# One-hots marked in batches of 16 and 20 groups of columns, and tables stored with one run per partition, in a graph network on one Trainium2 core

## The chip, the core and the metric

The kernel runs on one core of one Trainium2 chip. The core has five engines with a queue each: TensorE (PE, matmuls, with its weight loads listed as PEld), VectorE (DVE), ScalarE (ACT), GpSimd (POOL) and SyncE (SP), which here only issues DMAs. SBUF has 128 partitions. The metric is the device time of one execution in microseconds (us); the time before is a median of 3 runs.

## The reference

A graph of N = 6250 nodes with 128 values each has E = 206,250 directed edges (100,000 in both directions, and one from each node to itself). Two networks run one behind the other:

```
# first network, 2 layers (l = 0, 1); row, col = the edge's two ends
m   = relu(concat(h[row], h[col]) @ msg_W1[l].T + msg_b1[l]) @ msg_W2[l].T + msg_b2[l]
agg = segment_sum(m, col, num_segments=N)
h   = layer_norm(h + concat(h, agg) @ upd_W[l].T + upd_b[l])
# second network, 3 layers; src, dst = the edge's ends
agg = segment_sum(h[src], dst, num_segments=N) / max(deg, 1)
h   = agg @ Wl[i].T + bl[i] + h @ Wr[i].T          # relu between layers
```

Around each stand a layer norm of the input, a relu and a residual sum.

## The kernel before

The nodes lie in SBUF as 50 tiles of P = 125 rows: node t*125 + p is in partition p, tile t. First the edges are **sorted** (0 to 590 us) into slots: for a target tile, up to 32 x 13 slots in each of four row groups hold the edges whose target is there. Then come five edge stages, with short dense stages between them that make the next tables. `Fori` is a hardware loop; a semaphore makes an engine wait until a count is reached.

**Edge stages of the first network** (functions `cells_*`, lines L1190 to L1423; l = 0 from about 635 us, l = 1 from about 1411 us). Their source tables `TABH` lie in SBUF in float16. Each of the 50 target tiles is visited twice in a layer (h = 0 with 6 positions of slots, h = 1 with 7), 200 visits in all. For a visit SyncE loads the tile's lists of slots (`lists`, L1202) and the target rows of that tile (`stack`, L1208). VectorE compares lists with row numbers (`by_node`: L1395 for the 125 source rows into `toN`, L1396 for 64 rows that stand for target rows into `toB`) and slots with columns (`by_slot`, L1404). ScalarE copies the target rows into `cur` (`own_rows`, L1363). TensorE gathers (L1326 from `TABH`, L1330 from `cur`), ScalarE applies the relu (L1377), TensorE scatters (L1344) and VectorE adds the sums (L1412; `sums(0, ...)` for the first half of a visit's positions, `sums(1, ...)` for the second). `toB` and `cur` have 96 rows, of which 64 are used; GpSimd clears the other 32 at the start of each layer (L1276), and TensorE waits for that by `f_one`.

The target rows go through DRAM. While the last tables are made, in five blocks c of 10 tiles, SyncE stores for each block the target rows (L1220, to `rows_stacked`) and the source rows (L1222, to `table_a`, from which GpSimd later gathers the rare edges that found no slot). In block 2 it also loads the target rows of the first two tiles. Its queue is in order, so the lists of the third tile (L1202) are asked for after the stores of block 4.

**The first edge stage of the second network** (functions `linear_*` and `counts_dve` with l = 0, lines L1440 to L1656, 2214 to 2730 us). One iteration takes two target tiles, 100 cells of 125 x 125 (a cell: how many edges go from one source tile to the target tile). The 100 cells are 25 groups of 4 (`GROUP`, positions 0 to 24; tile u = 1 starts at position 12). For each group VectorE makes two one-hots of 4 x 126 columns (`onehots`, L1590, from `curS2` and the constants `col1` and `colg`), TensorE multiplies them to counts (`count`, L1518), ScalarE copies these to float16 (L1580), TensorE multiplies them with the table (`total`, L1538), and SyncE stores them for the two later layers (L1443). The one-hots have RING = 5 buffers of one group. After the last group of a tile VectorE takes the sums (`sums`, L1610, L1613, L1603): those of tile u = 1 at position 4 of the next iteration, those of u = 0 at position 17. GpSimd copies the slots of the next tile to `curS2` (`own_slots`, L1479 and L1481), gathers the rows of rare edges (`far_rows`, L1487 and L1489) that TensorE adds at positions 12 and 24 (`far_total`, L1526), and after its loop adds a bias to all of X for a later stage (L2133, five instructions). 

**The two later layers** (2772 to 3075 and 3108 to 3430 us) load the stored cells again; TensorE multiplies them with the table (L1551).

The functions that the change touches:

## Time and profile before

| what | value |
|---|---|
| median of the 3 runs (3422.79 to 3432.80) | 3429.53 us |
| profiled execution | 3434.72 us, of which the span of its instructions 3433.0 us |
| mean granted TensorE clock | 0.93 |
| PE / DVE / ACT / POOL busy | 86% / 75% / 60% / 18% of the span |
| first network, l = 0 and l = 1 | about 635 to 1320 us and 1411 to 2070 us |
| second network, l = 0, 1, 2 | 2214 to 2730, 2762 to 3076, 3107 to 3430 us |

Busy time is a union of instructions, and TensorE's matmuls overlap each other by most of their length; how fast an engine goes is read from the distance of starts. A releaser behind "<-" is what ended an engine's idle time; "issue" is idle time in which the profile shows nothing waited for.

### The profile page before, as it was taken

What the parts mean: (1) busy time and instruction counts of PE and PEld (TensorE: products, weight loads), DVE (VectorE), ACT (ScalarE), POOL (GpSimd) and SP (SyncE); (2) the same over time, 40 slices, a digit from 0 to 9 for tenths busy, and PEclk for the clock granted to TensorE, in tenths of its full rate; (3) what the DMA queues carried; (4) which work ended last, traced back from release to release, by engine and by line L of the source; (5) the groups of instructions that cost most, each with busy time, mean ns of one, the idle gap of its engine ahead of it and who ended that gap; (6) DMA issues with size and microseconds to landing.
All of it is one profiled execution on the core that took longest, in us unless ns stands there. A gap on an engine that the chain in (4) does not pass through costs nothing.

```text
span 3433.0 us, 220197 instructions
## 1 busy us (share of the span) xinstructions
PE 2955.7 (86%) x88775; PEld 2730.1 (80%) x88775; DVE 2576.5 (75%) x5711; ACT 2069.9 (60%) x3898; POOL 619.9 (18%) x914
## 2 busy tenths in 40 slices
PE   3665665599999998799999997798998799999999
PEld 2554544499988887699988886688888799999999
DVE  6899998677767776677766675799999865556555
ACT  1333333577767776777766775677777555555555
POOL 1211113400011116300011116122222300000000
PEclk7777776799999999899999999899999899999999
DMA  3000000566656662466656563255555478877888
GB/s 69 9 6 6 6 6 20 141 184 183 184 162 174 176 176 76 140 184 185 188 162 171 172 173 61 62 168 165 167 166 165 132 230 266 266 232 228 271 258 253
DMA packets 445075, 518.81 MB, mean 151 GB/s; under 512 B 153683, under 2 KB 321013, under 8 KB 444994
## 3 DMA queue, kind: packets, MB, share of 16 engines
q1 hardware_dynamic: 415959, 499.02, 48.6%
q0 software_dynamic: 4000, 8.20, 2.0%
q10 hardware_dynamic: 25035, 10.60, 1.2%
q8 instruction: 39, 0.64, 0.1%
q14 instruction: 42, 0.34, 0.0%
HBM read 408.98 MB, written 108.65 MB: 151 GB/s over the span
## 4 chain that ended last, share of the span: by engine, by line
PE 70%; DVE 12%; issue 8%; SPq 2%; POOL 2%; DMA 2%; ACT 2%; DVEq 0%; ACTq 0%; POOLq 0%
PE psum L1326 19%; PE psum L1551 17%; PE psum L1344 9%; PE psum L1330 9%; PE psum L1538 6%; PE psum L1518 4%; DVE arena L1590 2%; PE psum L691 1%; PE psum L1526 1%; DVE Hf L929 1%; POOL arena L2026 1%; DVE AGGf L974 1%; POOL tabf L2009 1%; DVE Hf L1068 1%; DVE Hf L2113 1%
## 5 line engine op out<-in xcount | busy, mean ns | idle before, releaser
L1326 PE MATMUL psum<-tabf,arena 125*32 125x128 f16 x40256 | 1105.7, 220 | 68.5 <-issue 27.5
L1326 PEld LDWEIGHTS psum<-tabf,arena 125*32 125x32 f16 x40256 | 953.3, 97 | 144.3 <-issue 100.7
L1330 PE MATMUL psum<-arena 96*32 96x128 f16 x20928 | 1045.3, 221 | 9.5 <-issue 9.5
L1377 ACT ACTIVATE arena<-psum 128x512 f32<-128x512 f32 x1300 | 776.4, 597 | 374.4 <-PE psum L1330 352.6
L1330 PEld LDWEIGHTS psum<-arena 96*32 96x32 f16 x20928 | 701.9, 95 | 12.0 <-issue 7.2
L1551 PE MATMUL psum<-tabr,cellr 125*125 125x256 f32 x5000 | 626.6, 285 | 5.6 <-ACT cellr L1473 5.5
L1551 PEld LDWEIGHTS psum<-tabr,cellr 125*125 125x125 f32 x5000 | 609.2, 188 | 6.9 <-issue 6.8
L1344 PE MATMUL psum<-arena 128*32 128x129 f32 x10400 | 566.0, 277 | 0.4 <-issue 0.4
L1473 ACT CAST cellr<-arena 125x630 fp32r<-125x630 f16 x500 | 359.7, 720 | 270.4 <-PE psum L1551 241.0
L1580 ACT CAST arena<-psum 125x500 f16<-125x500 f32 x625 | 360.8, 578 | 154.5 <-PE psum L1518 117.7
L1473 DVE CAST cellr<-arena 125x630 fp32r<-125x630 f16 x500 | 244.0, 488 | 244.3 <-PE psum L1551 240.4
L1538 PE MATMUL psum<-tabf,arena 125*125 125x256 f16 x2500 | 380.9, 275 | 0.2 <-ACT arena L1580 0.2
L1412 DVE TENSOR_TENSOR AGGf<-AGGf,psum 125x129 f32 x404 | 117.2, 290 | 303.1 <-PE psum L1344 302.8
L1518 PE MATMUL psum<-arena 128*125 128x125 bf16 x2508 | 255.5, 225 | 62.0 <-DVE arena L1590 38.6
L1518 PEld LDWEIGHTS psum<-arena 128*125 128x125 bf16 x2508 | 218.2, 139 | 81.0 <-DVE arena L1590 46.0
L1590 DVE TENSOR_TENSOR arena<-col,arena 128x504 bf16<-128x504 bf16 x627 | 269.6, 430 | 1.2 <-POOL arena L1481 1.0
L1538 PEld LDWEIGHTS psum<-tabf,arena 125*125 125x125 f16 x2500 | 265.4, 139 | 0.5 <-ACT arena L1580 0.5
L1344 PEld LDWEIGHTS psum<-arena 128*32 128x32 f32 x10400 | 256.6, 110 | 11.0 <-issue 1.7
L1590 DVE TENSOR_TENSOR arena<-colg,arena 128x504 bf16<-128x504 bf16 x627 | 264.6, 422 | 0.0
L1363 ACT COPY arena<-tabf 64x512 f16<-64x512 f16 x402 | 243.1, 605 | 27.7 <-DMA tabf<-rows_stacked 27.4
L1284 POOL COPY ovcur<-ovidx 128x1 int32 x50 | 28.5, 570 | 1178.6 <-PE psum L1330 1178.6
L1404 DVE TENSOR_TENSOR arena<-col,to_slots 128x384 f32<-128x384 bf16 (+1 forms) x404 | 236.4, 585 | 0.2 <-issue 0.2
(313 smaller groups left out, 4405.8 us busy)
## 6 DMA issues: line engine op xcount, KB each, us to landing
arena<-cells_kept SPq DMA_DIRECT2D x500, 315.0 KB
cells_kept<-arena SPq DMA_DIRECT2D x625, 126.0 KB, 1.7
arena<-slots_turned_from SPq DMA_DIRECT2D x152, 384.0 KB
tabf<-slots_turned_from SPq DMA_DIRECT2D x150, 384.0 KB, 3.4
arena<-slots_turned_from SPq DMA_DIRECT2D x50, 512.0 KB
tabf<-slots_turned_from SPq DMA_DIRECT2D x50, 512.0 KB
arena<-slots_turned_to SPq DMA_DIRECT2D x152, 96.0 KB
tabf<-slots_turned_to SPq DMA_DIRECT2D x150, 96.0 KB, 3.9
```

Of the source, the lines that this page charges most:

```text
L1326: pe.matmul(psCell[b][q:q + GW, g * D:(g + 1) * D], fr, rows, start=g == 0 and p == 0, stop=False, tile_position=(0, q), skip_group_check= ...
L1330: m = pe.matmul(psCell[b][q:q + GW, g * D:(g + 1) * D], toB[part][:, here + q:here + q + GW], cur[:, part, g, :], start=g == 0 and 4 * k + ...
L1344: m = pe.matmul(psA[half][q:q + GW, 0:W], toE[half][:, pos - 3 * half, g, :], msgs[:, SLOT[pos], g, 0:W], start=first, stop=pos == part_en ...
L1363: act.copy(cur[0:CP * GW, half], stack_in[u]).then_inc(f_cur[half], 1)
L1377: act.activation(msgs[:, SLOT[pos], :, 0:D], psCell[SLOT[pos]].rearrange("p (c d) -> p c d", d=D), ACT.Relu).then_inc(f_msg, 1)
L1404: dve.tensor_tensor(toE[half][:, 0:count], col1[:, 0:GW].rearrange("p (o u e) -> p o u e", o=1, u=1).to_broadcast(grid), to_slots[:, :, at ...
L1473: copy(cells_r[:, q % UNIT_RING], held.rearrange("p (c e) -> p c e", c=UNIT)).then_inc(l_cast[e], 1)
L1518: m = pe.matmul(psMsg[b][0:P, c * P:(c + 1) * P], oneE[:, b, c, 0, 0:P], oneE[:, b, c, 1, 0:P], start=True, stop=True, skip_group_check=True)
L1538: m = pe.matmul(psA[u][0:P, 0:LP * D], cells[0:P, pos % RING, c, 0:P], TABL[:, t].rearrange("p c d -> p (c d)"), start=t == 0, stop=t == N ...
L1551: m = pe.matmul(psA[u][0:P, 0:2 * D], cells_r[:, q % UNIT_RING, k, 0:P], TABR[:, first + k].rearrange("p c d -> p (c d)"), start=first + k ...
L1580: act.copy(cells[0:P, pos % RING, :, 0:P], psMsg[pos % RING][0:P, 0:GROUP * P].rearrange("p (c d) -> p c d", d=P)).then_inc(l_Cc, 1)
L1590: o = dve.tensor_tensor(pairs(oneE[:, pos % RING, :, a, :]), columns(numbers, 126, GROUP), along(curS2[:, pos * GROUP:(pos + 1) * GROUP, a ...
```

## The change

It has six parts.

1. **One-hots by batch.** `MARKED = [4, 4, 4, 4, 4, 5]` groups make a batch: 6 batches for the 25 groups, 12 VectorE instructions of 16 x 126 or 20 x 126 columns in place of 50 of 4 x 126. The one-hots now have MARKS = 3 buffers of a whole batch. TensorE waits once for a batch. GpSimd's copies wait for batch 5 and batch 3.
2. **Later sums.** `sums` of tile u = 1 stands behind batch 2 (groups 8 to 11), that of u = 0 behind batch 5.
3. **Stacked table in 128 rows.** `rows_stacked` is [128, 50, 256], and one store of a block takes 128 partitions with 5120 contiguous bytes each. The load of a tile's target rows becomes two DMAs of 32 x 4 x 128, and partitions are numbered in the order of (half, row).
4. **Tables by row.** The source rows go to a new `rows_far`, and the H rows to `rows_of_h`, with node p*50 + t at row (p, t), so a partition writes one contiguous run; the source rows' store is cut into 112 and 13 partitions. The indices of the rare edges are computed for that order.
5. **VectorE clears the unused rows** of `toB` and `cur`, behind its first `by_node` and `by_slot`, in place of GpSimd. The three spare rows of the stacked table are cleared once in SBUF by GpSimd at the start of the program (32 partitions x 6400 float32), in place of a DMA.
6. SyncE waits for the last sum of the second network's first stage before it loads stored cells, since the larger one-hots now lie where these are loaded.

```diff
+MARKED = [4, 4, 4, 4, 4, 5]
+MARKS = 3
-        oneE = carve([128, RING, GROUP, 2, 126], BF16)
+        oneE = carve([128, MARKS, max(MARKED) * GROUP, 2, 126], BF16)
...
-                sp.dma_start(stack_in[w], stack_dram[at].rearrange("o (g i) (c d) -> (o i c) g d", g=RG, c=CP)).then_inc(f_stk[w], 16)
+                for c in range(CP):
+                    sp.dma_start(stack_in[w][c * GW:(c + 1) * GW], stack_dram[:, at, c * D:(c + 1) * D].rearrange("(g i) o d -> (o i) g d", g=RG)).then_inc(f_stk[w], 16)
...
-                sp.dma_start(stack_dram[c * TB:(c + 1) * TB, 0:P].rearrange("t q e -> q t e"),
-                             TABH[:, 1, c * TB:(c + 1) * TB].rearrange("q t c d -> q t (c d)")).then_inc(f_stack[c // 2], 16)
-                sp.dma_start(table_dram[0].rearrange("(t p) d -> p t d", p=P)[:, c * TB:(c + 1) * TB, :],
-                             TABH[:, 0, c * TB:(c + 1) * TB].rearrange("p t c d -> p t (c d)")).then_inc(f_table, 16)
+                sp.dma_start(stack_dram[:, c * TB:(c + 1) * TB].rearrange("q t e -> q (t e)"),
+                             TABQ[:, 1, c * TB:(c + 1) * TB].rearrange("q t e -> q (t e)")).then_inc(f_stack[c // 2], 16)
+                for a, b in ((0, WIDE), (WIDE, P)):
+                    sp.dma_start(far_dram.rearrange("(p t) d -> p t d", p=P)[a:b, c * TB:(c + 1) * TB, :].rearrange("p t d -> p (t d)"),
+                                 TABH[a:b, 0, c * TB:(c + 1) * TB].rearrange("p t c d -> p (t c d)")).then_inc(f_table, 16)
...
-            for n, unused in enumerate((toB[0], toB[1], cur)):
-                pool.memset(unused[CP * GW:STACKED], 0.0).then_inc(f_one, 1)
-                hold(pool, "pool", f_one, l * 4 + (n + 1))
...
+                if h == 0:
+                    for unused in (toB[0], cur, toB[1]):
+                        dve.memset(unused[CP * GW:STACKED], 0.0).then_inc(f_one, 1)
...
-                pe.wait_ge(l_from, group_done(i, l, pos, 2))
+                n = batch_of(pos % BODY)
+                if pos % BODY == BEGIN[n]:
+                    pe.wait_ge(l_from, marked(i, n + BATCH * (pos // BODY)))
...
-                dve.wait_ge(l_C, before_it(i, l, pos, RING, 2))
+                dve.wait_ge(l_C, group_done(i, l, BEGIN[n - MARKS + 1] - 1 if n >= MARKS else BEGIN[n - MARKS + 1 + BATCH] - 1 - BODY))
...
-                for pos in range(BODY):
-                    onehots(i, pos)
+                for n in range(BATCH):
+                    onehots(i, n)
...
-                    if pos == 4:
-
+                    if n == 2:
                         sums(i, bass.ds(i * 2, 1), 1, -1)
-                    if pos == LAST[0] + 5:
+                    if n == batch_of(LAST[0]) + 2:
                         sums(i, bass.ds(i * 2 + 1, 1), 0, LAST[0])
...
+            pool.memset(tabf[P // 32 * 32:128, NT * D:NT * 2 * D], 0.0).then_inc(f_pad, 1)
```

**VectorE in the loop of the second network's first stage, before.** The rows are its instructions in program order, from position 3 to position 6 (line, operation, tile written <- tiles read, shape).

```order
L1590 TENSOR_TENSOR arena<-col,arena 128x4x126
L1590 TENSOR_TENSOR arena<-colg,arena 128x4x126
L1588 REGISTER_ALU
L1590 TENSOR_TENSOR arena<-col,arena 128x4x126
L1590 TENSOR_TENSOR arena<-colg,arena 128x4x126
L1610 ISA
L1610 SCALAR_TENSOR_TENSOR acc<-Hf,selfs,psum 125x128
L1613 TENSOR_TENSOR acc<-acc,psum 125x128
L542 REGISTER_ALU
L1603 ISA
L1603 SCALAR_TENSOR_TENSOR AGGf<-acc,invdegs,AGGf 125x128
```

The same engine and place in the changed kernel, from batch 1 to batch 3.

```order
L1613 TENSOR_TENSOR arena<-col,arena 128x16x126
L1613 TENSOR_TENSOR arena<-colg,arena 128x16x126
L1611 REGISTER_ALU
L1613 TENSOR_TENSOR arena<-col,arena 128x16x126
L1613 TENSOR_TENSOR arena<-colg,arena 128x16x126
L1633 ISA
L1633 SCALAR_TENSOR_TENSOR acc<-Hf,selfs,psum 125x128
L1636 TENSOR_TENSOR acc<-acc,psum 125x128
L549 REGISTER_ALU
L1626 ISA
L1626 SCALAR_TENSOR_TENSOR AGGf<-acc,invdegs,AGGf 125x128
```

Between two sums there stood 24 or 26 one-hots of 504 columns; now there stand 6 of 2016 or 2520, and the sum comes 12 groups after the tile's start in place of 5.

**SyncE while it stores the tables of the first network, before**: block 2 to the lists of the third tile.

```order
L1220 DMA rows_stacked<-tabf 125x10x256
L1222 DMA table_a<-tabf 125x10x256
L1208 DMA tabf<-rows_stacked 64x4x128 x2
L1220 DMA rows_stacked<-tabf 125x10x256
L1222 DMA table_a<-tabf 125x10x256
L1220 DMA rows_stacked<-tabf 125x10x256
L1222 DMA table_a<-tabf 125x10x256
L1202 DMA arena<-slots_turned_from 128x1536
```

The same place in the changed kernel.

```order
L1236 DMA rows_stacked<-tabf 128x2560
L1239 DMA rows_far<-tabf 112x2560
L1239 DMA rows_far<-tabf 13x2560
L1224 DMA tabf<-rows_stacked 32x4x128 x4
L1236 DMA rows_stacked<-tabf 128x2560
L1239 DMA rows_far<-tabf 112x2560
L1239 DMA rows_far<-tabf 13x2560
L1236 DMA rows_stacked<-tabf 128x2560
L1239 DMA rows_far<-tabf 112x2560
L1239 DMA rows_far<-tabf 13x2560
L1217 DMA arena<-slots_turned_from 128x1536
```

The order of the steps is kept; three runs of 2560 float16 per partition stand where two stores of ten rows of 256 per partition stood, and the loads of target rows are four in place of two.

## Rows read from the trace of the kernel before

**Rows 1.** Windows: start:end, length, busy us, granted clock, DMA share, GB/s.

```profile
680.00:1390.00 710.00, 678.07 (x35798) 629.01 (x35791) 514.14 (x929) 509.50 (x962) 110.33 (x140) 0.98 0.57 163
2216.00:2708.00 492.00, 442.11 (x5015) 423.96 (x5014) 471.51 (x1428) 355.55 (x616) 142.09 (x252) 1.00 0.51 165
```

**Rows 2.** Waits between 2240 and 2700 us: total, times, longest.

```profile
PE psum L1518 <- issue: 23.3, 24, 1.0
PE psum L1518 <- DVE arena L1590: 22.3, 23, 1.0
```

**Rows 3.** Timeline of PE in that stage: start, length, instruction.

```profile
2451.29 0.40 PE L1518 MATMUL psum<-arena 128*125 128x125 bf16 x4
...
2451.96 0.40 PE L1518 MATMUL psum<-arena 128*125 128x125 bf16 x4
```

**Rows 4.** Timeline of DVE at the same place.

```profile
2447.81 0.34 DVE L1610 SCALAR_TENSOR_TENSOR acc<-Hf,selfs,psum 125x128 f32<-125x128 f32 x1
...
2449.10 0.41 DVE L1590 TENSOR_TENSOR arena<-col,arena 128x504 bf16<-128x504 bf16 x1
2449.43 0.41 DVE L1590 TENSOR_TENSOR arena<-colg,arena 128x504 bf16<-128x504 bf16 x1
```

**Rows 5.** PE's far_total at position 24: first iteration, 24th and last.

```profile
2237.21 0.43 PE L1526 MATMUL psum<-ovrow,ovone 128*125 128x128 f32 x2
...
2693.74 0.43 PE L1526 MATMUL psum<-ovrow,ovone 128*125 128x128 f32 x2
...
2728.45 0.44 PE L1526 MATMUL psum<-ovrow,ovone 128*125 128x128 f32 x2
```

**Rows 6.** Timeline of DVE in the sort: two longer one-hots.

```profile
308.06 2.31 DVE L929 TENSOR_TENSOR Hf<-col,arena 128x2000 bf16<-128x2000 bf16 x2
```

**Rows 7.** Timeline of POOL in one iteration; from the page, gather's us to landing.

```profile
2237.90 1.13 POOL L1487 COPY ovcur<-ovidx 128x1 int32 x1 [10.57 <-PE psum L1526]
2239.82 0.97 POOL L1489 DMA_INDIRECT ovrow<-rows_of_h,ovcur  x1 [0.79 <-POOL ovcur L1487]
...
ovrow<-rows_of_h,ovcur POOLq DMA_INDIRECT x75, 4.1
```

**Rows 8.** Timelines of POOL, DVE and PE at the end of that stage.

```profile
2704.61 15.00 POOL L2133 TENSOR_TENSOR tabf<-tabf,bias 125x1280 f32<-125x1280 f32 x5
2707.88 3.10 DVE L1590 TENSOR_TENSOR arena<-col,arena 128x504 bf16<-128x504 bf16 x1
2720.28 0.69 PE L1518 MATMUL psum<-arena 128*125 128x125 bf16 x4 [4.69 <-DVE arena L1590]
```

**Rows 9.** Timelines of PE, DVE, SP at the first network's start.

```profile
648.69 0.40 PE L1326 MATMUL psum<-tabf,arena 125*32 125x128 f16 x8 [17.13 <-ACT arena L1363]
635.83 0.62 DVE L1395 TENSOR_SCALAR arena<-arena,row 125x1536 f16<-125x1536 f16 x1 [2.21 <-POOL tabf L2009]
675.53 0.62 DVE L1395 TENSOR_SCALAR arena<-arena,row 125x1536 f16<-125x1536 f16 x1 [14.99 <-DMA arena<-slots_turned_to]
656.97 6.86 SPq L1222 DMA_DIRECT2D table_a<-tabf  x1
```

**Rows 10.** Window of the stores; columns as in rows 1.

```profile
660.00:670.00 10.00, 3.43 (x202) 3.01 (x188) 0.54 (x2) 1.21 (x3) 0.00 (x0) 0.87 0.36 107
```

**Rows 11.** First network, l = 1: timelines of DVE and PE at its start.

```profile
1411.76 0.62 DVE L1395 TENSOR_SCALAR arena<-arena,row 125x1536 f16<-125x1536 f16 x1 [1.11 <-POOL tabf L2009]
1418.49 0.41 PE L1326 MATMUL psum<-tabf,arena 125*32 125x128 f16 x8 [9.88 <-POOL arena L1278]
```

**Rows 12.** ACT's copies that free and need a buffer of target rows.

```profile
903.00 0.61 ACT L1363 COPY arena<-tabf 64x512 f16<-64x512 f16 x1
...
911.69 0.61 ACT L1363 COPY arena<-tabf 64x512 f16<-64x512 f16 x1
```

**Rows 13.** Chain that ended last, before the second network's layer l = 1.

```profile
2761.32 3.91 DMA rows_of_h<-Hf
```

**Rows 14.** Timeline of POOL at the program's start: a clear of 512 float32.

```profile
1.62 0.52 POOL L2256 MEMSET abias<- 125x512 f32 x1
```

More of the change, by code:

```diff
@@ L51 @@
 RING = 5
+MARKED = [4, 4, 4, 4, 4, 5]
+BATCH = len(MARKED)
+MARKS = 3
+BEGIN = [sum(MARKED[:n]) for n in range(BATCH + 1)]
 KEPT = 10
@@ L1131, in group_done, with batch_of, marked @@
             return i * BODY + (BODY + k * (PAIRED * BODY + extra) + pos + 1)
+        def batch_of(pos):
+            return max(n for n in range(BATCH) if BEGIN[n] <= pos)
+        def marked(i, n):
+            return i * BATCH + (BODY + n + 1)
         def before_it(i, k, pos, buffers, extra=0):
@@ L1366, in cells_act @@
             act.wait_ge(m_low, (l + 1) * DUOS)
-            own_rows(0, 0, 16 * (l * (NT + 1) + 1), visit_base(2 * l) + ahead(2 * l, 2))
+            own_rows(0, 0, 32 * (l * (NT + 1) + 1), visit_base(2 * l) + ahead(2 * l, 2))
             for h in range(2):
@@ L1504, in linear_pool @@
                 if l == 0:
-                    hold(pool, "pool", l_from, group_done(i, l, -1, 2))
+                    hold(pool, "pool", l_from, marked(i, -1))
                     own_slots(bass.ds(i * 2 + 1, 1), 1)
-                    hold(pool, "pool", l_from, group_done(i, l, LAST[0], 2))
+                    hold(pool, "pool", l_from, marked(i, batch_of(LAST[0])))
                     own_slots(bass.ds(i * 2 + 2, 1), 0)
@@ L1583, in counts_dve, with onehots @@
         def counts_dve(dve, l):
-            def onehots(i, pos):
+            def onehots(i, n):
                 for u in range(2):
-                    if pos == FIRST[u]:
+                    if n == batch_of(FIRST[u]):
                         dve.wait_ge(l_own, i * 2 + (l * (NT + 1) + u + 1))
-                dve.wait_ge(l_C, before_it(i, l, pos, RING, 2))
+                dve.wait_ge(l_C, group_done(i, l, BEGIN[n - MARKS + 1] - 1 if n >= MARKS else BEGIN[n - MARKS + 1 + BATCH] - 1 - BODY))
                 for a, numbers in enumerate((col1, colg)):
-                    o = dve.tensor_tensor(pairs(oneE[:, pos % RING, :, a, :]), columns(numbers, 126, GROUP),
-                                          along(curS2[:, pos * GROUP:(pos + 1) * GROUP, a, :], 126), ALU.is_equal)
+                    o = dve.tensor_tensor(pairs(oneE[:, n % MARKS, 0:MARKED[n] * GROUP, a, :]), columns(numbers, 126, MARKED[n] * GROUP),
+                                          along(curS2[:, BEGIN[n] * GROUP:BEGIN[n + 1] * GROUP, a, :], 126), ALU.is_equal)
                 o.then_inc(l_from, 1)
@@ L2300, in _ @@
             pool.sem_inc(l_unit, UNIT_RING)
-            pool.memset(to_slots[:, :, NT, :], 0.0)
-            pool.memset(selfs[:, 0:1], 0.0)
+            pool.memset(to_slots[:, :, NT, :], 0.0).then_inc(f_pad, 1)
+            hold(pool, "pool", f_pad, 1)
+            pool.memset(selfs[:, 0:1], 0.0).then_inc(f_pad, 1)
+            hold(pool, "pool", f_pad, 2)
+            pool.memset(tabf[P // 32 * 32:128, NT * D:NT * 2 * D], 0.0).then_inc(f_pad, 1)
+            hold(pool, "pool", f_pad, 3)
             def prepare_weights():
@@ L2423, in _ @@
             dve.wait_ge(s_const, 1)
-            step.did(dve.tensor_scalar(row32[:], row1[0:CP * GW], 0.5, -0.75, ALU.mult, ALU.add))
-            step.last()
-            step.did(dve.tensor_scalar(row32[:], row32[:], MAGIC, None, ALU.add))
-            step.last()
-            step.did(dve.tensor_scalar(row32[:], row32[:], MAGIC - 1.0, None, ALU.subtract))
+            for b in range(CP):
+                step.did(dve.tensor_scalar(row32[b * GW:(b + 1) * GW], row1[b * GW:(b + 1) * GW], float(b * GW), None, ALU.subtract))
             for g in range(RG):
```

49 lines of the change are left out of this document (25 added, 24 removed).

## The prediction

> **What bounds the kernel now.** I read the share of time by stage first (windows), then who waits for whom, then the timelines where an engine idles. In the edge stages of the first network TensorE is busy for 678 of 710 us, at its full 2.4 GHz nearly throughout [rows 1]; nothing in the change makes its matmuls fewer, so little can be won inside. The stage that differs is the second network's first: TensorE 442 of 492 us, VectorE 471 [rows 1]. The reader is to see two engines of nearly equal speed and a stall between them. Inside a tile TensorE's groups follow each other in 0.67 us [rows 3], VectorE's pairs of one-hots in 2 x 0.33 = 0.66 us [rows 4]. When VectorE takes a tile's sums, 1.29 us pass between its one-hots [rows 4], the five buffers are not refilled, and TensorE waits: 45.6 us in all [rows 2]. Iterations of two tiles last (2693.74 - 2237.21) / 23 = 19.85 us, and the last one 34.71 us [rows 5]. The second place is where the first network starts: TensorE stands still for 17 us, and later VectorE for 15 us, since the lists of the third tile are asked for only behind stores that hold SyncE for up to 6.86 us each [rows 9].
>
> **One-hots by batch, later sums (parts 1, 2).** A pair of one-hots of 2000 columns takes 2.31 us in the sort [rows 6]. An instruction of 504 is listed with 0.41 us and followed after 0.33, an overlap of 0.08 [rows 4]; with the same overlap the longer ones follow each other in (2.31 - 0.08) / 2 = 1.115 us. The slope between the two sizes is (1.115 - 0.33) / 1496 = 0.525 ns a column, the fixed part 0.067 us. So 2016 columns take 1.12 us and 2520 take 1.39. An iteration has ten of the first and two of the second: 14.0 us, where 50 x 0.33 = 16.5 stood. Two sums are 2.6 us. What is left of today's 19.85 us, 0.75, is the one-hots of rare edges and collisions with GpSimd, and stays: VectorE needs 17.35 us.
>
> TensorE needs 25 x 0.67 = 16.75 us, plus what remains of 19.85 when its stalls of 45.6 / 23.2 = 1.97 us an iteration are off: 1.1 us, which holds the rare edges' matmuls (these stay) and the slow groups after each stall (these go). So its own pace is 17.3 to 17.9 us. The two engines stay level, but up to twelve groups of one-hots are ahead in place of five, so that a sum of 1.29 us (two groups) is covered. I take 17.6, between TensorE's ends: 23 x 2.25 = **52 us** for the iterations with a steady neighbour. Ends: 17.3 gives 59, and 18.5 (first rival) gives 31.
>
> The Trainium skill (VectorE: DVE Perf Modes, The TRN2 errata) says that an instruction with an SBUF source pays a fixed extra per instruction, that small tiles pay it each, and advises 512 elements or more. By it the step from 504 to 2016 would be worth almost nothing; the rows here give 38 fewer fixed parts of 0.067 us, 2.5 us an iteration, and I go by the rows.
>
> The first iteration starts later by what a batch takes more than a group, 2 x (1.12 - 0.33) = 1.6 us, and loses its two stalls of about 1 us: zero.
>
> The last iteration is 34.71 us because GpSimd, through with its loop, runs five instructions of 3 us [rows 8], and while they run a one-hot takes 3.10 us in place of 0.41; TensorE waits for that, once for 4.69 us [rows 8]. After the change GpSimd is free when batch 3 is marked. Four one-hot instructions (batch 5 and the batch behind the loop) then each stand behind one of GpSimd's, about 2.7 us plus their own 1.1 to 1.4. Batch 4 slips by before. The last batch is ready 15.6 to 18 us after batch 3. TensorE, 4 to 12 groups into the iteration by then, has 13 to 21 groups of 0.67 us to do first, 8.7 to 14.1 us, and waits for 1.5 to 9 us. I take 4.6: 17.6 + 4.6 = 22.2, a gain of **12.5 us** (8 to 16).
>
> **Stores of one run per partition, stacked table (parts 3, 4).** Before: in the window of the stores the DMA engines are busy for 0.36 and move 107 GB/s [rows 10], so most of them stand idle. The five blocks are 6.25 MB, 58 us at this rate. Elsewhere the kernel moves 165 GB/s at a share of 0.51 [rows 1], 320 at a full one. With the engines fully used a block's stores take about 4 us, and SyncE is free within some 5 us of the last table, which is done when VectorE goes on at 635.83 [rows 9]. At 165 GB/s a block takes 7.6 us, and the lists of the third tile would come about 7 us late.
>
> The Trainium skill (DMA: Bandwidth & Descriptors, Why a DMA increments its semaphore by 16 and not by 1) says that a DMA is split over the largest number of engines up to 16 that divides both sides' slowest dimension. 125 rows would get 5 engines, and 128 or 112 get 16; the share of 0.36 is near 5 of 16, so the trace agrees.
>
> What follows for l = 0: TensorE starts at 648.69 now [rows 9]. VectorE starts its comparisons at 635.83 [rows 9]. TensorE needs one such comparison of 0.62 us [rows 9], and five instructions more: the second comparison, the one-hots by slot and the three new clears, for which VectorE has no row. I bound a clear by nothing and by 0.62 us, and take 0.62 for each of the five: 3.7 us, so TensorE starts at 639.5, 9.2 us earlier. Then the wait of 14.99 us for the lists [rows 9] goes, and with it about 1 us of halved clock behind it: **25 us** in all. Ends: 18, if the lists still come 7 us late; 28, if the clears cost nothing and the clock stays up.
>
> For l = 1 the tables come slower and the stores are hidden but for the last. VectorE starts at 1411.76, TensorE at 1418.49 behind GpSimd's clears [rows 11]; by the same 3.7 us it starts at 1415.4, 3.1 us earlier: **3 us** (2 to 7, the top if a standstill or two behind it go as well).
>
> The loads of target rows, two in place of one, cost SyncE 0.15 to 0.6 us a visit. They are hidden: the copy that frees the buffer ends at 903.6, the one that needs it starts at 911.7 [rows 12], 8.1 us for a load. Without the cover each us late costs 200 us, once a visit.
>
> H rows by row: before the layer l = 1 of the second network a store of 3.91 us is on the chain [rows 13]; a faster one gives **1 us** (0 to 2). For the two other layers the gather is needed later, and it is hidden.
>
> **Clears and the wait (parts 5, 6).** GpSimd clears 512 float32 in 0.52 us at the start [rows 14], so 6400 take 6.5 us, from 10 us on. If VectorE's first conversions were held until the clear ends, 4 us would be lost. I take 0, since the clear only writes and VectorE waits for its input at first. SyncE's wait (part 6) ends when the last sum does, 30 us before the next layer starts [rows 5, 13]: 0.
>
> **Sum.** 52 + 12.5 + 25 + 3 + 1 = 93.5 us. The profiled execution took 3434.7 and goes to 3341.2; against the median of 3429.5, 5.2 lower, I expect **3336 us**.
>
> **Rivals.**
> - *GpSimd comes too late.* Its gather is issued 2.6 us after TensorE's last use [rows 5, 7] and lands 4.1 us later [rows 7]: 6.7 of the 12 x 0.67 = 8.0 us that TensorE will leave. Its 1.13 us copy already waits for VectorE [rows 7]. If two GpSimd instructions wait for a whole one-hot of 1.12 us each, the rows land at 8.5 or later, and copies of slots for tile u = 1 hold batch 3 too. Price: an iteration of 18.5, 21 us lost, 3357 us. The Trainium skill (SBUF — State Buffer) says that VectorE with two SBUF inputs and GpSimd reading SBUF exclude each other for a whole instruction, which speaks for this rival. Against: when VectorE is ahead it waits, and GpSimd is free. Chance 0.2.
> - *The stores stay slow*, bound by DRAM: of the 25 us only the earlier start stays, 9: 3352 us. Against: 165 GB/s elsewhere [rows 1]. Chance 0.07.
> - *Slower: strided target rows.* Each partition row is now 25,600 bytes from the next in DRAM. If a load took over 8.1 us, every visit would wait; at 8.6 us it costs 200 x 0.5 = 100 us and eats the gain; at 9 us, 180 us and 3516 us. The same number of pieces of 256 bytes speaks against. Chance 0.04.
> - *The change brings nothing*, as VectorE's fixed part does not shrink and TensorE waits as before, and gains and losses cancel: chance 0.02.
>
> **How the numbers follow.** The forecast has 0.67, with its own range 3318 to 3350: the best ends, 59 + 16 + 28 + 7 + 2 = 112 us, and 80 us when steady iterations are 17.9 and the start gives 20. All low ends together, 31 + 8 + 18 + 2 + 0 - 4 = 55 us, give 3374. I take 3315 to 3370. A difference of 0.3%, 10 us, is about what a measurement of this kernel tells from no change. Faster: 0.93; within: 0.02; slower: 0.05.
>
> **What would show it.** In the profile after: iterations of 17.6 us between the matmuls of rare edges, with no wait of TensorE for the one-hots; VectorE's one-hots 1.12 us apart; the last iteration near 22 us. At the first network's start TensorE from about 639.5 us and no wait of VectorE for lists; a DMA share well over 0.36 while tables are stored. The prediction is wrong if TensorE waits for the gathered rows or batch 3 in each iteration, or ScalarE waits for target rows in each visit.

## The result, and the profile after

The changed kernel takes 3352.45 us, the median of four runs (3351.78 to 3353.03); the kernel before, beside it, 3428.31 us (four runs, 3422.79 to 3432.8). The ratio is 0.9775, with a 95% interval of 0.9764 to 0.9787: faster by 76 us. In the profiled executions the span went from 3433.0 to 3351.3 us, 81.7 us less, at a mean granted clock of 0.932.

In the changed file the one-hots are L1613 (before L1590), the counting matmuls L1541, the summing matmuls L1561, the rare edges' matmuls L1549, ScalarE's copy of counts L1603, the store of that copy to DRAM L1460, GpSimd's copies of slots L1499 and L1501, its copy of the gather's index L1507, the sums L1633, L1636 and L1626, the comparison by node L1409, the new clears L1436.

**The second network's first layer.** The rare edges' matmuls of the second tile, in the first, 24th and last iteration, as in [rows 5]:

```profile
2210.05 0.44 PE L1549 MATMUL psum<-ovrow,ovone 128*125 128x128 f32 x2
...
2621.88 0.44 PE L1549 MATMUL psum<-ovrow,ovone 128*125 128x128 f32 x2
...
2645.48 0.69 PE L1541 MATMUL psum<-arena 128*125 128x125 bf16 x4 [6.29 <-DVE arena L1613]
...
2647.24 0.73 PE L1549 MATMUL psum<-ovrow,ovone 128*125 128x128 f32 x2
```

A steady iteration takes (2621.88 - 2210.05) / 23 = 17.91 us where 19.85 stood, the last one 25.36 where 34.71 stood; TensorE still stands once for 6.29 us in it. The waits between 2210 and 2620 us, beside [rows 2]:

```profile
POOL arena L1499 <- DVE arena L1613: 70.3, 23, 3.3
ACT arena L1603 <- DMA cells_kept<-arena: 16.9, 17, 1.3
DVE arena L1613 <- POOL arena L1501: 13.6, 10, 1.4
PE psum L1561 <- ACT arena L1603: 4.9, 12, 0.6
```

The rows of before with 45.6 us of TensorE are gone; TensorE's own waits above 0.15 us are 6.0 us here. What is left reads in two chains: ScalarE waits for stores of counts that have not landed, and TensorE for ScalarE; VectorE waits for GpSimd's copies of slots. VectorE's one-hots in this stage, by form (count, busy us, mean ns):

```profile
L1613 DVE TENSOR_TENSOR arena<-colg,arena 128x2016 bf16<-128x2016 bf16 x114 | 137.7, 1208 | 0.0
L1613 DVE TENSOR_TENSOR arena<-colg,arena 128x2520 bf16<-128x2520 bf16 x23 | 34.4, 1496 | 0.0
```

**The first network's start**, timelines of PE, DVE and SP's queue, beside [rows 9], and then the DMA engines while tables are stored (columns as in [rows 1]; before, the same 30 us had a share of 0.35 and 105 GB/s):

```profile
642.26 0.40 PE L1340 MATMUL psum<-tabf,arena 125*32 125x128 f16 x8 [8.28 <-DVE arena L1436]
...
637.67 0.62 DVE L1409 TENSOR_SCALAR arena<-arena,row 125x1536 f16<-125x1536 f16 x1 [1.38 <-POOL tabf L2031]
...
639.89 1.24 DVE L1436 MEMSET arena<- 32x768 uint32 x2 [0.21 <-issue]
641.29 0.91 DVE L1436 MEMSET arena<- 32x1024 uint32 x1 [0.16 <-issue]
...
638.00 1.38 SPq L1239 DMA_DIRECT2D rows_far<-tabf  x2
...
610.00:640.00 30.00, 18.69 (x68) 11.36 (x68) 27.49 (x42) 24.01 (x59) 25.48 (x22) 0.96 0.56 199
```

In the timeline of SyncE's queue no store holds it for more than 1.6 us, no wait of VectorE for lists is left, and TensorE starts 6.4 us earlier than in [rows 9]. At l = 1 it starts at 1393.31 us, 25.2 earlier than in [rows 11].

### The profile page after: what moved, and what is told of

It is laid out like the page before. It is cut to its first block, busy times and chain, and to the rows that moved or that the text cites. A ratio compares the mean times of both kernels' runs of the same rounds, so it can differ in the third digit from the quotient of the medians.

```text
span 3351.3 us, 219053 instructions
## 1 busy us (share of the span) xinstructions
PE 2939.6 (88%) x88775; PEld 2733.2 (82%) x88775; DVE 2504.7 (75%) x4764; ACT 2061.8 (62%) x3898; POOL 697.0 (21%) x909
## 4 chain that ended last, share of the span: by engine, by line
PE 71%; DVE 12%; issue 7%; DMA 3%; ACT 3%; POOL 2%; SPq 2%; DVEq 0%; POOLq 0%; ACTq 0%
PE psum L1340 19%; PE psum L1574 17%; PE psum L1358 9%; PE psum L1344 9%; PE psum L1561 6%; PE psum L1541 3%; PE psum L698 2%; DMA cells_kept<-arena 1%; PE psum L1549 1%; DVE Hf L2135 1%; DVE Hf L936 1%; POOL arena L2048 1%; PE psum L695 1%; DVE Hf L1075 1%; DVE AGGf L981 1%
## 5 line engine op out<-in xcount | busy, mean ns | idle before, releaser
L1340 PE MATMUL psum<-tabf,arena 125*32 125x128 f16 x40256 | 1098.5, 220 | 43.4 <-issue 26.7
L1603 ACT CAST arena<-psum 125x500 f16<-125x500 f32 x625 | 352.8, 580 | 101.4 <-PE psum L1541 43.7
L1561 PE MATMUL psum<-tabf,arena 125*125 125x256 f16 x2500 | 380.6, 275 | 6.6 <-ACT arena L1603 6.2
L1561 PEld LDWEIGHTS psum<-tabf,arena 125*125 125x125 f16 x2500 | 264.1, 138 | 9.5 <-ACT arena L1603 8.9
L1541 PE MATMUL psum<-arena 128*125 128x125 bf16 x2508 | 250.0, 222 | 12.9 <-DVE arena L1613 12.7
L1541 PEld LDWEIGHTS psum<-arena 128*125 128x125 bf16 x2508 | 228.9, 139 | 16.0 <-DVE arena L1613 15.4
L1410 DVE TENSOR_SCALAR arena<-arena,row 64x1536 f16<-64x1536 uint8 (+1 forms) x202 | 216.6, 1072 | 0.0
L1410 DVE TENSOR_SCALAR arena<-tabf,row 64x1536 f16<-64x1536 uint8 x200 | 214.4, 1072 | 0.0
```

The source lines that it names most:

```text
L1340: pe.matmul(psCell[b][q:q + GW, g * D:(g + 1) * D], fr, rows, start=g == 0 and p == 0, stop=False, tile_position=(0, q), skip_group_check= ...
L1410: dve.tensor_scalar(toB[half][0:CP * GW, span], slist[v][half][1][:, span], row32[:], None, ALU.is_equal).then_inc(f_toN, 1)
L1541: m = pe.matmul(psMsg[b][0:P, c * P:(c + 1) * P], oneE[:, n % MARKS, at, 0, 0:P], oneE[:, n % MARKS, at, 1, 0:P], start=True, stop=True, s ...
L1561: m = pe.matmul(psA[u][0:P, 0:LP * D], cells[0:P, pos % RING, c, 0:P], TABL[:, t].rearrange("p c d -> p (c d)"), start=t == 0, stop=t == N ...
L1603: act.copy(cells[0:P, pos % RING, :, 0:P], psMsg[pos % RING][0:P, 0:GROUP * P].rearrange("p (c d) -> p c d", d=P)).then_inc(l_Cc, 1)
```

## The experiments

A few per cent of the kernel's time hang on the chip: where the first comparison and the second set of experiments ran, the kernel before takes 3428 and 3434 us, in the first and third set 3394 and 3395. So times are compared within a set, and ratios to the kernel before across sets. Three sets of four kernels ran; each edit is against the changed kernel unless it says otherwise.

### Each part undone alone

**One-hots by group, old places of the sums**

```diff
-MARKED = [4, 4, 4, 4, 4, 5]
+MARKED = [1] * BODY
...
-MARKS = 3
+MARKS = 5
...
-                    if n == 2:
+                    if n == 4:
...
-                    if n == batch_of(LAST[0]) + 2:
+                    if n == LAST[0] + 5:
```

> The changed kernel with the one-hots of the second network's first linear layer made by group of four cells again (five buffers, sums behind groups 4 and 17), all other parts of the change kept. Theory: batching and later sums are the whole gain of that stage, so the steady iteration goes from 17.9 back to 19.8 us, the last from 25.4 to about 34.7, and the kernel is 54 us slower than the changed one, about 3406 us. Rival: part of the stage's gain came from the other parts (rows of H stored by row, so that the gather and the stores share the DMA engines better); then the iteration stays under 19.3 and the time under 3395 us.

Measured 3367.35 us, ratio 0.9922 (0.9903 to 0.9941). The rare edges' matmuls give 19.96 us an iteration and 33.64 for the last, and TensorE waits for one-hots again as in the kernel before (waits between 2171 and 2665 us, the last iteration included):

```profile
PE psum L1541 <- DVE arena L1613: 60.3, 50, 5.1
```

The stage gives back (19.96 - 17.91) x 23 + 8.3 = 55 us by its own landmarks; the ratios differ by 0.0127 to 0.0147 (by the changed kernel's 0.9795 in the second set and its 0.9775), 43 to 50 us of 3394. The theory stands, and the other parts gave this stage nothing, since 19.96 is no less than the 19.85 of before (3406 us in the expectation is for the chip of the first comparison).

**Target rows and rows of H by node**

```diff
-                for a, b in ((0, WIDE), (WIDE, P)):
-                    sp.dma_start(far_dram.rearrange("(p t) d -> p t d", p=P)[a:b, ...
+                sp.dma_start(table_dram[0].rearrange("(t p) d -> p t d", p=P)[:, ...
...
-                act.dma_start(rows_dram.rearrange("(p t) d -> p t d", p=P)...
+                act.dma_start(rows_dram.rearrange("(t p) d -> p t d", p=P)...
```

The indices of the rare edges go back to the order of nodes as well.

> The changed kernel with the tables of target rows and of H stored in the order of nodes again (a row of a node every tile, over 125 partitions), the stacked table kept in its 128 rows. Theory: these stores alone, half of the bytes, again take most of SyncE's time at the first network's start, and the lists of the third tile come late by about half of what they did: 5 to 9 us slower than the changed kernel, with TensorE's first matmul no later and VectorE waiting 4 to 8 us for lists; plus 0.6 us for the rows of H. Rival: one slow store of two hides under table making (7.2 us a block); then under 2 us.

Measured 3321.96 us, ratio 0.9781 (0.9765 to 0.9797), within 2 us of the changed kernel's 0.9775. The theory falls, the rival holds: the queue is held again, 8.26 us over four loads of stacked rows and 6.93 by a request for a list, but VectorE waits for no list.

**Stacked table by tile**

```diff
-        stack_dram = nc.dram_tensor("rows_stacked", [RG * GW, NT, CROW], ...
+        stack_dram = nc.dram_tensor("rows_stacked", [NT, RG * GW, CROW], ...
...
-                for c in range(CP):
-                    sp.dma_start(stack_in[w][c * GW:(c + 1) * GW], ...
+                sp.dma_start(stack_in[w], stack_dram[at].rearrange("o (g i) (c d) -> (o i c) g d", ...
```

> The changed kernel with the stacked table stored by tile again (125 rows and cleared spare rows by DMA, one load a visit), the target rows kept by row. Theory: as for the target rows, 5 to 9 us slower at the first network's start, less the conversion that the clear of the spare rows holds at the program's start (0 to 3 us): 2 to 9 us slower. A second thing that could show: two loads a visit in place of one cost SyncE and DMA something in every visit; if so this kernel wins back some us in the 100 visits of each layer. Rival: nothing, under 2 us.

Measured 3328.83 us, ratio 0.9806 (0.9789 to 0.9823): 10 us over 0.9775, 4 over the 0.9795 that the changed kernel had in the second set. Against 0.9795 the intervals overlap, so not even the sign is sure. One load a visit in place of two won nothing back: from TensorE's start at l = 0 to that at l = 1 this kernel takes 741.5 us, the one with target rows by node and two loads 731.8, and the two others of this set, with two loads as well, 736.8 and 737.0.

**Clears on GpSimd**

```diff
-                    for unused in (toB[0], cur, toB[1]):
-                        dve.memset(unused[CP * GW:STACKED], 0.0).then_inc(f_one, 1)
...
+            for n, unused in enumerate((toB[0], toB[1], cur)):
+                pool.memset(unused[CP * GW:STACKED], 0.0).then_inc(f_one, 1)
```

> The changed kernel with the three clears of unused rows on GpSimd again. Theory: TensorE's first cell matmul at the first network's start comes 8 us later (VectorE's comparison to TensorE took 12.9 us before and takes 4.6 now), at l = 1 by 2.1 us: 8 to 10 us slower. Rival: the clears were slow on GpSimd only because the comparisons that wait for lists stood between; then 2 to 4 us.

Measured 3324.84 us, ratio 0.9788 (0.9771 to 0.9804). GpSimd's timeline:

```profile
635.96 1.77 POOL L1293 MEMSET arena<- 32x1536 f16 x1 [0.25 <-POOL tabf L2031]
637.89 2.40 POOL L1293 MEMSET arena<- 32x2048 f16 x1 [0.15 <-POOL arena L1293]
640.45 1.15 POOL L1293 MEMSET arena<- 32x1024 f16 x1 [0.15 <-POOL arena L1293]
```

TensorE's idle time ahead of its first matmul is 10.4 us here and 8.3 in the changed kernel; at l = 1 it is 9.9 and 7.7: 2.1 us a layer. By these rows the rival holds; the times alone can't tell, since the interval holds both ratios of the changed kernel. The wait of 12.9 us between VectorE's comparison and TensorE's start in [rows 9] was not GpSimd's clears, it was ScalarE's copy behind the late loads.

**Both tables and the rows of H as before** (the diffs of the target rows and of the stacked table together; the clears stay on VectorE)

> The changed kernel with both tables, the rows of H, and the loads of the stacked rows as they were before (parts 3 and 4 undone together), one-hots by batch and clears on VectorE kept. Undone one at a time the two parts cost 0.06% (target rows) and 0.3% (stacked table), and neither brought VectorE's wait for the lists back. Theory: either store alone hides behind the making of the tables, both together do not; the wait for the lists of the third tile comes back, 12 to 15 us, and the ratio to the kernel before is 0.982 to 0.985, where the changed kernel has 0.9775 and 0.9795. Rival: the wait came from GpSimd's clears between, which are gone here; then TensorE runs through and the ratio is 0.979 to 0.981.

Measured 3346.95 us, ratio 0.9859 (0.984 to 0.9879), 22 to 29 us slower by the changed kernel's 0.9795 and 0.9775. Timelines of DVE and of SP's queue:

```profile
670.36 0.62 DVE L1407 TENSOR_SCALAR arena<-arena,row 125x1536 f16<-125x1536 f16 x1 [15.01 <-DMA arena<-slots_turned_to]
...
645.56 6.21 SPq L1235 DMA_DIRECT2D rows_stacked<-tabf  x1
651.81 6.88 SPq L1237 DMA_DIRECT2D table_a<-tabf  x1
658.79 5.79 SPq L1217 DMA_DIRECT2D arena<-slots_turned_from  x1
```

The wait for the lists is back with 15.01 us, where [rows 9] have 14.99, and TensorE stands still for 17.2 us until ScalarE's copy ends its wait, 17.13 in [rows 9]. On the same chip the next kernel, which has the new stores, makes its first comparison 5.1 us later than this one, and yet its TensorE starts l = 1 18.5 us earlier (1374.74 and 1393.21 us). Alone each half costs 0 to 10 us, together 22 to 29: the two stores stand one behind the other in one queue, and the time they are late for is passed only by both.

**Sums a batch earlier**

```diff
-                    if n == 2:
+                    if n == 1:
-                    if n == batch_of(LAST[0]) + 2:
+                    if n == batch_of(LAST[0]) + 1:
```

> The changed kernel with each tile's sums one batch of one-hots earlier (behind batches 1 and 4, where they stand behind 2 and 5). Theory: VectorE then reaches the sums before TensorE has finished the tile, since its buffers let it be 12 groups ahead; it waits there, and as its own pace (17.4 us) leaves no slack, the iteration grows from 18.0 to 18.3 to 18.9 us: 5 to 20 us slower. Rival: the wait falls into the time in which VectorE would wait for a buffer anyway; then nothing within 3 us.

Measured 3355.93 us, ratio 0.9882 (0.9862 to 0.9901). An iteration takes 19.39 us and the last one 30.39, worse than the theory's 18.9. The waits of the stage:

```profile
DVE acc L1633 <- PE psum L1561: 33.9, 46, 1.0
PE psum L1541 <- DVE arena L1613: 25.2, 23, 1.1
```

VectorE waits 46 times for a tile that TensorE has not finished, and TensorE 23 times for the one-hots that come behind. By the ratios 30 to 36 us go back, well over half of the 43 to 50 us that the one-hots and the sums bring together, though the batches are as long as in the changed kernel: most of what the long one-hots save VectorE goes into this wait.

### What the changed kernel still loses

**The changed kernel again**, on the chip of the next three.

> The changed kernel unaltered, on the chip of the three kernels below, as their comparison. Its ratio to the kernel before was 0.9775; if the gain doesn't hang on the chip, the ratio lies in 0.9764 to 0.9787 again, and steady iterations of the second network's first linear layer take 17.9 us, the last one 25.4 us.

Measured 3363.56 us against 3434.15, ratio 0.9795 (0.9779 to 0.9812). The ratio is just above the expected range; the intervals of the two sets overlap. The iteration is 18.20 us and the last 26.47, where 17.9 and 25.4 were expected: the waits below differ between executions (VectorE waits for GpSimd's slots 20.3 us here, 13.6 in the first), and the iteration of an unchanged stage lies between 17.91 and 18.20 us in the six kernels that have it.

**Nine buffers for the counts**

```diff
+STORED = 9
+HELD = [len(range(b, BODY, STORED)) for b in range(STORED)]
...
-        cells = carve([128, RING, GROUP, 126], F16)
+        cells = carve([128, STORED, GROUP, 126], F16)
...
-                    act.wait_ge(l_sum, before_it(i, l, pos, RING))
-                    act.wait_ge(l_keep[pos % RING], i * (16 * BODY // RING) + (16 * (pos // RING) + 16))
+                    act.wait_ge(l_sum, before_it(i, l, pos, STORED))
+                    act.wait_ge(l_keep[pos % STORED], i * (16 * HELD[pos % STORED]) + ...
```

> The changed kernel with nine buffers for the copied counts in place of five. ScalarE waited 16.9 us in 410 for stores of counts that had not landed (17 times). Theory: these waits cost TensorE part of what an iteration has over 17.2 us (25 groups of 0.667 us and two pairs of rare edges' matmuls at 0.27 us); the iteration goes from 17.9 to 17.5 to 17.7 us, 5 to 9 us less in all. Rival: ScalarE's wait is covered by the groups that are counted ahead, and the 0.7 us an iteration come from VectorE's wait for GpSimd's copies of slots (13.6 us in 410); then no change within 2 us.

Measured 3366.37 us, ratio 0.981 (0.9791 to 0.9828), no gain; the iteration is 18.37 us. ScalarE's wait for stores is gone, VectorE's for GpSimd has grown, and TensorE's for VectorE with it. Waits between 2211 and 2633 us, and one round of GpSimd's timeline:

```profile
DVE arena L1616 <- POOL arena L1504: 24.5, 18, 1.4
...
PE psum L1544 <- DVE arena L1616: 17.1, 17, 1.1
...
2412.20 3.02 POOL L1510 COPY ovcur<-ovidx 128x1 int32 x1 [5.42 <-PE psum L1552]
2416.03 0.96 POOL L1512 DMA_INDIRECT ovrow<-rows_of_h,ovcur  x1 [0.81 <-POOL ovcur L1510]
2416.99 0.28 POOL L1502 COPY arena<-tabf 128x96 bf16 x1
2417.20 0.20 POOL L1504 COPY arena<-tabf 128x4 bf16 x1
```

GpSimd's copy of one index takes 3.02 us beside one-hots that follow each other without a gap, and the copies of slots that batch 3 needs stand behind it. Both the theory and its rival had a piece: the rival names the wait that remains, but the first wait was real, as the next two kernels show: without nine buffers it comes through to TensorE, and with them and the slots first the iteration is shorter than with either alone.

**Slots ahead of the rare edges' rows**

```diff
-                far_rows(i)
                 if l == 0:
                     hold(pool, "pool", l_from, marked(i, -1))
                     own_slots(bass.ds(i * 2 + 1, 1), 1)
+                far_rows(i)
```

> The changed kernel with GpSimd's copy of the slots of the second tile ahead of its work for the rare edges' rows in each iteration, where it is behind it. Theory: the copy then is done up to 5 us earlier, while TensorE finishes the last tile, batch 3 waits no more (VectorE waited 1.4 us there, 10 times in 23), and the iteration goes from 17.9 to 17.5 to 17.7 us, 5 to 9 us less. Rival: the copies now stand ahead of the gather, held by one-hots of 1.12 us each, the gathered rows come late for TensorE, and the iteration gets longer, up to 18.5 us (14 us more).

Measured 3358.14 us, ratio 0.9775 (0.9759 to 0.9791): 5 us under the changed kernel beside it, within the intervals. Iterations of 17.98 us, the last 22.81. VectorE's wait for GpSimd is gone; ScalarE's for the stores stays and now comes through to TensorE:

```profile
ACT arena L1604 <- DMA cells_kept<-arena: 15.5, 14, 1.6
...
PE psum L1562 <- ACT arena L1604: 9.1, 20, 0.8
```

**Both, and GpSimd's additions of a bias behind the last batch**

```diff
             if l == 1:
+                hold(pool, "pool", l_from, marked(PAIRED, 0))
                 for c in range(NB_LOOPS):
                     pool.tensor_tensor(X[:, block_of(c), :], ...
```

> The changed kernel with nine buffers, the slots before the rows, and GpSimd's five additions of a bias (16 us, which hold the last iteration's one-hots) started only when the last batch of one-hots is marked. Theory: VectorE's own pace of 17.4 us (14.0 of one-hots, two sums of 1.5, rare edges 0.4) bounds the steady iteration, so 17.4 to 17.5 in place of 17.9: 9 to 12 us; the last iteration goes from 25.4 to 18.5 to 20 us, 5 to 7 us: 14 to 19 us faster than the changed kernel, a ratio to the kernel before of 0.972 to 0.973. Rival: the additions then hold VectorE's last sums and the next layer's start instead, and 2 to 4 us of the last iteration's gain are given back.

Measured 3336.09 us, ratio 0.9719 (0.9702 to 0.9735): 27.5 us faster than the changed kernel beside it, more than the first two edits brought singly (3 us lost, 5 won, both within noise); the third was not run alone. The window of the steady iterations:

```profile
2220.00:2600.00 380.00, 379.94 (x4451) 379.53 (x4451) 357.66 (x439) 310.96 (x546) 168.22 (x221) 1.00 0.58 189
```

TensorE is busy for 379.94 of 380 us. An iteration takes 17.42 us, 0.78 under the 18.20 beside it, and the last one 17.43 in place of 26.47: 17.9 + 9.0 = 26.9 us. Of the 9.0 the slots first bring 3.7 (22.81 us in the kernel above). The additions now run beside the making of the next tables, where one instruction of VectorE takes 2.04 in place of 0.41 us; the rival's price is under 2 us.

**The same with the spare rows cleared by DMA**

```diff
+                sp.dma_start(tabf[P:128, NT * D:NT * 2 * D].rearrange("p (n d) -> p n d", d=D),
+                             zrow[0:128 - P, 0:D].rearrange("p (o d) -> p o d", o=1).to_broadcast([128 - P, NT, D])).then_inc(f_pad, 16)
...
-            pool.memset(tabf[P // 32 * 32:128, NT * D:NT * 2 * D], 0.0).then_inc(f_pad, 1)
```

> The kernel of nine buffers, slots first and late additions (ratio 0.9719), with the spare rows of the stacked table cleared by a DMA of zeros into SBUF in place of GpSimd's 5.4 us instruction at the start. The kernel without that instruction had the end of the sort 1.5 us earlier on the same chip and made its tables 1.4 us faster. Theory: VectorE's first conversion takes 0.2 in place of 3.0 us, the first network starts 1.5 to 3.5 us earlier: ratio 0.9708 to 0.9715, which the profile tells better than the times. Rival: the sort ends no earlier; same ratio.

Measured 3287.9 us (five runs), ratio 0.9688 (0.9668 to 0.9708), the lowest of all, though the interval touches that of 0.9719 (0.9702 to 0.9735). The conversion takes 0.20 us again, but the last step of the sort stands at 591.76 us, and at 591.85 in the kernel below, which has GpSimd's clear: the rival holds, the 3 us go under before the sort ends. That this ratio lies below 0.9719 isn't the DMA's work as far as the profile tells.

**Ten batches of 2 and 3 groups, five buffers** (against the kernel with nine buffers, slots first, late additions)

```diff
-MARKED = [4, 4, 4, 4, 4, 5]
+MARKED = [2, 3] * 5
...
-MARKS = 3
+MARKS = 5
...
-                    if n == 2:
+                    if n == 4:
...
-                    if n == batch_of(LAST[0]) + 2:
+                    if n == 9:
```

> The kernel of nine buffers, slots first and late additions, with ten batches of 2 and 3 groups in five buffers in place of six of 4 and 5 in three; the same 12 groups ahead. Theory (a fixed part of 0.067 us an instruction, 0.525 ns a column): a pair of 2 groups takes 2 x 0.596 us, of 3 groups 2 x 0.861; five of each make 14.6 us in place of 14.0, VectorE needs 18.0 us an iteration in place of 17.43, and the kernel is 13 us slower than that one, ratio 0.9757. Rival: batches are worth their size only as buffers; then the iteration stays at 17.4 to 17.5 us and the ratio at 0.972.

Measured 3304.33 us, ratio 0.9728 (0.9709 to 0.9748); iteration 17.63 us, last 17.92. VectorE's timeline:

```profile
2305.39 0.68 DVE L1617 TENSOR_TENSOR arena<-col,arena 128x1008 bf16<-128x1008 bf16 x1
2305.99 0.68 DVE L1617 TENSOR_TENSOR arena<-colg,arena 128x1008 bf16<-128x1008 bf16 x1
2306.58 0.94 DVE L1617 TENSOR_TENSOR arena<-col,arena 128x1512 bf16<-128x1512 bf16 x1
2307.44 0.94 DVE L1617 TENSOR_TENSOR arena<-colg,arena 128x1512 bf16<-128x1512 bf16 x1
2308.29 0.68 DVE L1617 TENSOR_TENSOR arena<-col,arena 128x1008 bf16<-128x1008 bf16 x1
```

Instructions of 1008 columns follow each other in 0.60 us, of 1512 in 0.86. The durations are as expected; the iteration is 0.4 us shorter than the 18.0 of the expectation, of which two sums with the gaps behind them are 0.2: they take 2.8 us where I had set 3.0. VectorE waits for nobody in it, so its own pace sets the iteration, 0.2 us over the 17.42 of the kernel it is compared with and 0.3 over the 17.34 of the one above. Against that last one, on the same chip, it is 14 to 16 us slower, of which these iterations hold 6.6. TensorE's share of the difference shows where it stands still (waits between 2176 and 2581 us, of which the list has those over 0.15 us):

```profile
PE psum L1553 <- DMA ovrow<-rows_of_h,ovcur: 1.2, 4, 0.4
```

From start to start, the rare edges' matmuls come late 15 times in 23 iterations, 4.0 us in all, each time 0.12 us after the gathered rows have landed; the one-hots are late 6 times, 1.3 us in all. So with VectorE never idle GpSimd's gather is what TensorE meets first, as in the prediction's first rival.

## Why the prediction was right, and where its terms were off

The forecast was 3336 us, its range 3315 to 3370, and 3352.45 lies in it; it lies just outside the narrower 3318 to 3350, to which the forecast gave 0.67. The cause was the right one in both places: one-hots and sums in the one stage, the late lists in the other. The sum of 93.5 us came out as 81.7 in the profiled execution, term by term:

- **Steady iterations, 52 us: measured 44.7** (23 x 1.94). The estimate of VectorE's one-hots held to a hundredth: 1.12 us a one-hot of 2016 columns, 1.38 to 1.39 of 2520, and the fixed part of 0.067 us with 0.525 ns a column also gives the sizes between. TensorE's own pace was taken as 17.3 to 17.9 and is 17.34 to 17.42, as the kernels without its waits show. The step that failed is that with up to twelve groups ahead the stalls are off. Two small ones stayed, and with them the iteration is 17.91 us in this execution and 18.20 in that of the same kernel on the other chip, between the 17.6 of the sum and the 18.5 of the first rival. One is that rival, in a mild form: GpSimd's short copies wait for several one-hots in a row. The other I had not seen: ScalarE waits for the stores of the counts, which mostly land in 1.7 us, but beside the gather in 2.3 us in the middle and in up to 3.6; nine buffers in place of five take this wait away. Taking away either one alone brings at most 5 us of the kernel's time, both together 17.9 in these iterations.
- **Later sums.** I had them as a detail of the batches. With long batches and the sums a batch earlier an iteration is 19.39 us, so of the 2.05 us between 19.96 and 17.91 the batches alone bring 0.6, and the later place then 1.5. That does not make the place worth more than the length. In the kernel before, VectorE waits for nothing but its own sum in the steady iterations (waits between 2237 and 2694 us):

```profile
DVE AGGf L1603 <- DVE acc L1613: 11.7, 46, 0.3
```

 So its own work, 19.85 us an iteration, was the bound, and TensorE's stalls followed from it. From start to start its one-hots take 16.8 us an iteration there and 13.9 in the changed kernel; that is the gain, and early sums spend half of it in a wait for TensorE. Short one-hots with late sums were not run; by VectorE's pace of 19.85 us, an estimate, they would bring next to nothing. The reading that a step beyond 504 columns is worth almost nothing is refuted by the same figures.
- **The last iteration, 12.5 us: measured 9.35.** One-hots of 3.89 and 3.88 us beside GpSimd's additions are what was worked out (2.7 + 1.1), and TensorE waits 6.29 us where I took 4.6, within 1.5 to 9. But only two one-hots were held so, and one instruction of a sum (2.64 us), where I had four one-hots. GpSimd was not free when batch 3 was marked: its copy of slots ended only at 2634.34 us, behind batch 5, and the additions began at 2634.77. The last batch was ready 16.4 us after batch 3, within the 15.6 to 18 worked out; two errors cancelled there, and that is luck. With the slots first and the additions later, the iteration takes 17.43 us; with the slots first alone it takes 22.81, so the later additions, with the nine buffers beside them, bring 5.4 us.
- **The first network's start, 25 us: measured 21 to 23.** TensorE starts 6.4 us earlier and not 9.2: the last table is 1.84 us later, and from VectorE's comparison to TensorE it takes 4.6 us in place of 3.7 (the clears are 1.24 us for two and 0.91, with gaps of 0.21 and 0.16, and the second comparison is 1.01, where I had 0.62 for each). The wait of 15 us goes as forecast. Undoing all the stores shows it from the other side. What I had not worked out is that either half of the stores would have done nearly as well.
- **l = 1, 3 us: measured 2.1 at its start** (VectorE 23.0 us earlier, TensorE 25.2). In the layer 6 more us are won (TensorE's cell matmuls span 651.2 us in place of 657.4), but the same kernel on the other chip takes 656.9, so the change does not bring them as far as is shown. Some 4 to 5 are lost again before the rare edges' matmuls of the second network's first iteration. No experiment takes these apart; they stay open.
- **H rows by row, 1 us: at most 0.5.** From the last rare edges' matmuls of the second network's first layer to the end the kernel takes 704.0 us where 704.5 stood; the store on the chain takes 3.31 us in place of 3.91. With 2.0 us won between TensorE's start at l = 1 and the first iteration, the terms are 23.0 + 2.1 + 2.0 + 44.7 + 9.35 + 0.5 = 81.7 us.
- **The clear at the program's start, 0 us: right in size, wrong in its reason.** I took VectorE to be free since the clear only writes. It isn't:

```profile
10.45 5.43 POOL L2322 MEMSET tabf<- 32x6400 f32 x1 [0.15 <-POOL selfs L2320]
...
12.76 3.16 DVE L883 CAST Hf<-Hf 125x50 f32<-125x50 int32 x1 [4.06 <-DMA Hf<-in_dst]
```

 The conversion ends at 15.92 us and the clear at 15.88. The conversion takes 0.20 us in the kernel before, in the two kernels without the stacked table in rows and in the one with the DMA. The Trainium skill (SBUF — State Buffer, Who interferes with whom) says that copies and casts of VectorE can enter a mode that holds the port pair it shares with GpSimd, and that the one that comes second is blocked for the whole instruction of the first; the trace agrees. The 3 us are gone by the end of the sort, so that the 0 held is luck.
- **Rivals.** Slow stores: refuted by 199 GB/s in the window of the stores. Strided target rows: refuted, ScalarE's waits in the visits of both layers are for TensorE alone, none for a load of target rows. No effect: refuted.

## What to carry to other kernels

When two engines run nearly level, look first for the one that waits for nobody: here it was VectorE, and its own work had to get shorter (12 long instructions in place of 50) for the stage to get shorter. Then look for what the partner needs next and how far ahead the engine is allowed to be: the 1.3 us of a sum, placed a batch too early, took back 1.5 of the 2.05 us that were won. After such a stall is removed, look for small ones that hid behind it and behind each other: here two single edits showed nothing clear of noise, and their combination 17.9 us. Work of GpSimd that nobody waits for had a price where VectorE was busy (one-hots of 3.9 in place of 1.2 us), so start it in a stage where VectorE has time.

## What the runs showed of the hardware that was not expected

- A GpSimd instruction can last as long as several instructions of VectorE, not only one. A copy that elsewhere takes 0.25 to 0.28 us took 4.95 us beside four one-hots that follow each other after 1.12 and 1.38 us, and ended when they did (timeline of POOL, changed kernel):

```profile
2629.39 4.95 POOL L1499 COPY arena<-tabf 128x96 bf16 x1 [3.32 <-DVE arena L1613]
2634.29 0.18 POOL L1501 COPY arena<-tabf 128x4 bf16 x1
```

- Chips differ in TensorE's short stops. Where the kernel before takes 3428 to 3434 us, TensorE stands 44 to 53 times at the cell matmuls of the first network for mostly 0.46 to 0.50 us with nothing that releases it (26.7 to 32.8 us in all, five changed kernels and the one before); where it takes 3394 us, 3 to 5 times (3.7 to 10.0 us, eight kernels). That is some 20 of the 33 to 40 us between the chips; what causes it the profile doesn't show.
- The table making ahead of the first network, from VectorE's first addition of a bias to its first comparison by node, takes 35.8 to 36.0 us in four of the kernels (the one before, the one-hots by group, the stacked table by tile, and all stores as before) and 37.1 to 37.5 in the others. No one part of the change tells the two apart. In the longer ones four or five of VectorE's 24 subtractions of 0.66 us take 0.93. This stays open.
